# Coupling phase rewritten: twice-projected first state, two sequences in step, outputs by diagonal gate matmuls, steps placed by a table

## The reference, cut to what matters

```python
h = _layernorm(x) * (1 + cb) + sb
gf = _global_net(h.mean(axis=1))                 # per sequence one number, three small layers
out = h
for _ in range(3):                               # NUM_CYCLES
    tf = sigmoid(gelu(gelu(gelu(out @ w1 + b1) @ w2 + b2) @ w3 + b3) @ w4 + b4)   # 256 -> 256 -> 128 -> 64 -> 1
    coupling = 0.1 + r * ((0.7 * gf + 0.3 * tf) - 0.5) * 2.0      # one number per token
    o_r, o_i, p_r, p_i = split(out, 4)
    out = out + coupling * concatenate([p_r, -p_i, -o_r, o_i])    # the twist
x = x + gb * out
```

## Time and profile before

| | us |
|---|---|
| median of 3 runs (1328.81 to 1330.93) | 1330.33 |
| the profiled execution's own time | 1328.92 |
| its span, first to last instruction | 1327.0 |
| coupling phase in it, from the end of the last linear-attention add at 1066.8 | 260.2 |

### The profile page before, as it was taken

The page is one execution under the profiler, slowest core; times in us unless marked ns, Lnnn a source line. Parts: engine busy times, 40 slices in busy tenths (PEclk is TensorE's granted clock), DMA queues, the critical chain, the costliest instruction groups (busy, mean ns, idle before and its releaser), DMA issues. The chain is left out here.

```text
span 1327.0 us, 19347 instructions
## 1 busy us (share of the span) xinstructions
PE 1121.3 (84%) x6462; PEld 593.2 (45%) x6462; DVE 744.3 (56%) x1538; ACT 566.0 (43%) x1025; POOL 457.4 (34%) x668
## 2 busy tenths in 40 slices
PE   6279999999999991598989638999999929999996
PEld 5134445554544430354545315666666613333332
DVE  3167778788787745223223237777777623464543
ACT  0227676676776661123223213333333204545543
POOL 0345446445454310478877523222223100000000
PEclk7669999999999995699999859999999969999997
DMA  4134134233252213266666430111110020012000
GB/s 169 30 58 77 26 70 93 46 75 85 39 90 58 43 50 105 72 128 155 130 151 132 75 99 1 37 37 37 37 41 17 21 91 1 8 56 64 0 32 32
DMA packets 73042, 85.26 MB, mean 64 GB/s; under 512 B 12520, under 2 KB 67560, under 8 KB 72688
## 3 DMA queue, kind: packets, MB, share of 16 engines
q1 hardware_dynamic: 60656, 67.23, 19.8%
q0 software_dynamic: 12288, 16.79, 7.7%
HBM read 45.54 MB, written 25.47 MB: 54 GB/s over the span
## 5 line engine op out<-in xcount | busy, mean ns | idle before, releaser
L655 DVE TENSOR_REDUCE nmax<-psum 128x1 f32<-128x512 f32 (+3 forms) x352 | 215.5, 636 | 51.9 <-PE psum L847 46.5
L759 ACT ACTIVATE pT<-psum 128x512 f32<-128x512 f32 x320 | 181.1, 596 | 66.7 <-PE psum L866 36.6
L845 PE MATMUL psum<-k6T,q6T 96*128 96x512 bf16 (+3 forms) x512 | 128.2, 310 | 14.3 <-DVE nmax L655 10.2
L863 PE MATMUL psum<-q6T,k6T 99*128 99x512 bf16 x320 | 119.4, 382 | 1.1 <-ACT pT L759 0.9
L1084 POOL DMA_INDIRECT residual<-expert_y,idx_e x64 | 101.2, 1581 | 37.6 <-DVE expert_y L1206 21.1
L2029 PE MATMUL psum<-c_state,c_w 128*128 128x512 f32 x192 | 102.5, 636 | 0.1
L847 PE MATMUL psum<-negs_bf,ident_bf 128*128 128x128 bf16 (+2 forms) x352 | 88.8, 252 | 0.0
L845 PEld LDWEIGHTS psum<-k6T,q6T 96*128 96x128 bf16 x512 | 45.7, 99 | 88.0 <-DVE nmax L655 55.5
L878 PE MATMUL psum<-pT,v 128*32 128x512 f32 x640 | 85.1, 604 | 0.0
L1487 DVE TENSOR_TENSOR l_scores<-psum,const_sb 128x512 f32<-128x512 f32 x128 | 79.1, 679 | 10.0 <-PE psum L1639 10.0
L1071 POOL DMA_INDIRECT expert_tokens<-router_input,idx_e x64 | 63.7, 995 | 54.3 <-POOLq L947 35.2
(11 more groups left out here) (234 smaller groups left out, 2259.1 us busy)
## 6 DMA issues: line engine op xcount, KB each, us to landing
q6T<-q_parts SPq DMA_DIRECT2D x96, 128.0 KB, 4.5
expert_w<-in_ew SPq DMA_DIRECT2D x16, 768.0 KB
x_in<-in_x SPq DMA_DIRECT2D x8, 512.0 KB, 4.0
residual<-x SPq DMA_DIRECT2D x32, 128.0 KB, 1.8
router_input<-h SPq DMA_DIRECT2D x32, 128.0 KB, 1.8
l_x<-residual SPq DMA_DIRECT2D x8, 512.0 KB, 4.2
x_dram<-l_x SPq DMA_DIRECT2D x32, 128.0 KB, 3.5
c_x<-x_dram SPq DMA_DIRECT2D x4, 1024.0 KB, 6.0
```

What stands on the lines that cost most here:

```text
L655: dve.tensor_reduce(nmax[:, i, u * nh:(u + 1) * nh], ps_s[:, n % SR, 0:nh * (i + 1) * P].rearrange("p (h k) -> p h k", h=nh), AX_X, ALU.ma ...
L759: act.activation(pT[:, n % PR].rearrange("p h t -> p (h t)"), ps_t[:, n % TR, :], ACT.Exp, scale=HD ** -0.5).then_inc(probs, 1)
L845: pe.matmul(out[:, a, :], q6T[0:6 * HD, b % 2, u * nh + a, i * P:(i + 1) * P], k6T[0:6 * HD, b % 2, 0:w], start=a == 0, stop=False, skip_g ...
L863: last = pe.matmul(out, k6T[:, b % 2, j * P:(j + 1) * P], q6T[:, b % 2, hg * 4:hg * 4 + 4, i * P:(i + 1) * P], start=True, stop=j < i)
```

## The change

Only the coupling phase changes (and shared helpers: `attention_order` becomes `placed_order`, with the same table and order for attention; the signals that GpSimd primed in setup are gone). What it does now, per pair:

- `PR`: the first state `h` is multiplied by `w1` and by a twisted copy of it, `w1[:, 1]`, once: 2 sequences x 2 weights x 2 output halves, two matmuls each. ACT drains each into `pr` (and for the plain one also applies the gelu into `a1`). The layer-1 input of cycles 1 and 2 is made from `pr` by DVE in `up` (one scale, two products, two sums per sequence), with no L1 matmul; between them `r2` prepares the base of the third cycle.
- `L3` and `L4` of both sequences are issued together, on the two column halves and the two row halves of the array.
- `tok`: the coupling numbers are computed per token on partitions (four matmuls of two columns per cycle), `fin` turns them into alpha and beta of the third state by eleven small DVE operations.
- `oT`: for each of 8 token tiles, four real matmuls of the first state against diagonal gate matrices (`diag`, written by ACT), which transpose, gate and twist at once; DVE scales by alpha and beta and adds x.
- `xn` moves from DVE to ACT, and POOL gets two more small operations for its bias. The last cycle has no `L4` and no `up`.
- Steps stand where a table puts them, one period of 48 places per pair, and pairs overlap; there is no loop.

```diff
-def half_cycle(c1, a1, c2, a2, first=False, second=False):
-def coupling_prologue():
-def coupling_merged():
-class CouplingSignals:
+COUPLING_STEPS = 48
+COUPLING_PLACE = {
+    "ln": -143, "st": -136, "xn": -132, "diag": -116,
...
+}
@@ SP @@
+                        if q >= 3:
+                            sp.wait_ge(done, 2 * NT * (q - 2))
+                        sp.dma_start(x_in[:, q % 3], m.x3_d[...]).then_inc(in_loaded[q % 3], 16)
+                        if q == 0:
+                            (nine weight loads)
@@ POOL @@
+                        link(pool.tensor_scalar(vtmp[:], mv[:, :, 1], EPS, None, ALU.add))
+                        link(pool.tensor_tensor(rstd[:], vtmp[:], mhalf[:], ALU.pow))
+                        link(pool.tensor_tensor(vtmp[:], mv[:, :, 0], rstd[:], ALU.mult))
+                        pool.tensor_scalar(nbias[:], vtmp[:], -1.0, None, ALU.mult).then_inc(nbias_ready, 1)
@@ DVE @@
-                        chain.link(dve.tensor_scalar(cc[:, a, :], th[:, a, :], ...))
-                        dve.scalar_tensor_tensor(out=uv[:, a, 0, :], in0=st[:, 1, :], scalar=sgn, in1=cc[:, a, :], ...)
-                        chain.link(dve.scalar_tensor_tensor(out=uv[:, a, 1, :], in0=st[:, 0, :], scalar=nsgn[:, 0:1], ...))
-                        for k in range(KC):
-                            dve.tensor_tensor(st[:, k, :], st[:, k, :], uv[:, a, k, :], ALU.add)
+                        link(dve.tensor_scalar(cc[:, a, :], th[:, a, :], half[:, 2:3], coef[:, q % 2, a:a + 1], ALU.mult, ALU.add))
+                        dst = tmp[:] if c else pre[:, a]
+                        steps = [signed(dve.tensor_tensor(dst[:, k, :], pr[:, q % 2, a, 1, k, :], cc[:, a, :], ALU.mult))
+                                 for k in range(KC)]
+                        for k in range(KC):
+                            dve.wait_ge(dve_steps, steps[k])
+                            base = pre[:, a, k, :] if c else pr[:, q % 2, a, 0, k, :]
+                            dve.tensor_tensor(pre[:, a, k, :], base, dst[:, k, :], ALU.add).then_inc(pre_ready, 1)
+                    if s[0] == "r2":
+                        link(dve.tensor_tensor(tmp[:], pr[:, q % 2, a, 0], cc[...].to_broadcast([P, KC, T]), ALU.mult))
+                        link(dve.tensor_tensor(pr[:, q % 2, a, 1], pr[:, q % 2, a, 1], tmp[:], ALU.subtract))
+                    if s[0] == "oT":
+                        link(dve.scalar_tensor_tensor(out=ot[:, q % 2, n, :], in0=ps_o[:, n % 2, 0:C], scalar=al3[:, i, a:a + 1],
+                                                      in1=x_in[:, q % 3, n, :], op0=ALU.mult, op1=ALU.add))
+                        dve.scalar_tensor_tensor(out=ot[:, q % 2, n, :], in0=ps_o[:, n % 2, C:2 * C], scalar=be3[:, i, a:a + 1],
+                                                 in1=ot[:, q % 2, n, :], op0=ALU.mult, op1=ALU.add).then_inc(done, 1)
@@ ACT @@
+                        for i in range(2 * NT):
+                            ins = act.activation(xn[:, i, :], x_in[:, q % 3, i, :], ACT.Identity, bias=nbias[...], scale=rstd[...])
+                    if s[0] == "diag":     (eight of)
+                                act.activation(diag[:, q % 3, a, k, :], ident, ACT.Copy, scale=cols[:, 4 + k, a:a + 1])
+                    if s[0] == "PR":
+                        if w == 0:
+                            act.activation(a1[:, q % 2, a, h, :], src, ACT.Gelu, bias=bias[:, h:h + 1])
+                        act.activation(pr[:, q % 2, a, w, h, :], src, ACT.Copy).then_inc(pr_drain, 1)
@@ PE @@
-                        ins = pe.matmul(ps_1[:, a, h, :], w1[:, k, h * P:(h + 1) * P], o[:, q.s, a, k, :], ...)
+                            last = pe.matmul(ps_1[:, n % 2, :], w1[:, w, k, h * P:(h + 1) * P], o[:, q % 3, a, k, :], ...)
+                        for a in range(2):
+                            pe.wait_ge(l2, l2_use[("L2", q, c, a)] + 1)
+                            last = pe.matmul(ps_3[64 * a:64 * a + 64, :], w3[:], a2[:, a, :], tile_position=(0, 64 * a))
+                        for a in range(2):
+                            pe.matmul(ps_2[:, a, :], w4[64 * a:64 * a + 64, :], a3[64 * a:64 * a + 64, :], tile_position=(64 * a, 0))
+                        for i in range(NT):
+                            last = pe.matmul(ps_t[:, 2 * i:2 * i + 2], a3[:, i * P:(i + 1) * P], w4pair[:], start=True, stop=True)
-                                last = pe.transpose(ps_dve[...], og[:, a, k, ...], ident)
+                                last = pe.matmul(ps_o[:, n % 2, (KC * w + k) * P:(KC * w + k + 1) * P],
+                                                 o[:, q % 3, a, 1 - k if w else k, i * P:(i + 1) * P], diag[:, q % 3, a, KC * w + k, :])
```

More of the change, by code:

```diff
@@ L78, in shape_constants @@
     return c
[L81 to L104, removed]
 def settle(eng, passed):
     eng.sem_inc(passed, 1)
[L113 to L133, removed]
-S_HEADS = [4, 2, 1, 1]
[L148 to L160, removed]
+S_HEADS = [4, 2, 1, 1]
+ATTENTION_STEPS = 136
+ATTENTION_PLACE = {
     "ln": -197,
@@ L181, with placed_order, place @@
 }
+def placed_order(table, count, steps, sequences):
+    def place(s):
+        at = table[s[0]]
+        for n in s[1:]:
+            at = at[n]
+        return at
+    assert len(steps) == count
+    order = [(count * b + place(s), (s[0], b) + s[1:]) for b in range(sequences) for s in steps]
+    return [s for _, s in sorted(order)]
 def attention_steps():
@@ L1858, in _ @@
+                    if s[0] == "oT" and s[2] % 2:
+                        _, q, n = s
+                        sp.wait_ge(done, 2 * NT * q + n + 1)
+                        sp.dma_start(m.out_t[q * 2 * NT + n - 1:q * 2 * NT + n + 1].rearrange("i p c -> p i c"),
+                                     ot[:, q % 2, n - 1:n + 1]).then_inc(store[q % 2], 16)
+                for s in range(2):
+                    sp.wait_ge(store[s], 16 * NT * (R // 2))
             @block.gpsimd
             def _(pool):
-                chain = Chain(pool, g.pool_steps, m.passed)
@@ L1862, in step @@
[L1862 to L1871 removed]
+                count = [0]
@@ L1938, in _ @@
                 dve.tensor_scalar(half[:, 2:3], bias[:, 8:9], 0.3, None, ALU.mult)
[L1939 to L1942 removed]
+                dve.tensor_scalar(half[:, 3:4], bias[:, 8:9], 0.7, None, ALU.mult).then_inc(ready, 1)
+                dve.wait_ge(ready, 2)
+                for s in order:
+                    step(s)
@@ L1991, in _ @@
-                act.wait_ge(ready, 1)
-                program(act, step)
+                        _, q, c = s
+                        for a in range(2):
+                            act.wait_ge(l4_fill, 4 * q + 2 * c + a + 1)
+                            act.activation(th[:, a, :], ps_2[:, a, :], ACT.Tanh, bias=half[:, 0:1], scale=0.5).then_inc(l4, 1)
+                    if s[0] == "tok":
+                        _, q, c = s
+                        act.wait_ge(tok_fill, CYCLES * q + c + 1)
+                        if q:
+                            act.wait_ge(fin, q)
+                        act.activation(tht[:, c].rearrange("p i a -> p (i a)"), ps_t, ACT.Tanh, bias=half[:, 0:1],
+                                       scale=0.5).then_inc(tok, 1)
@@ new lines, in step @@
+                        last.then_inc(x_fill, 1)
+                    if s[0] == "g":
+                        if s[2] == 1:
+                            for k in range(KC):
+                                last = pe.matmul(ps_x[:, 0:2], g1w[:, k, :], sums[:, k, :], start=k == 0, stop=k == KC - 1)
+                        if s[2] == 2:
+                            last = pe.matmul(ps_x[0:64, 0:2], g2w[:], gs1[:], start=True, stop=True)
+                        if s[2] == 3:
+                            last = pe.matmul(ps_x[:, 0:2], g3w[:], gs2[:], start=True, stop=True)
+                        last.then_inc(x_fill, 1)
@@ L2065 @@
+                pe.wait_ge(ready, 2)
+                for s in order:
+                    step(s)
 INPUTS = {
```

545 lines of the change are left out of this document (283 added, 262 removed).

## The result

| | before | after |
|---|---|---|
| median of 4 runs each, us | 1330.37 (1328.81 to 1330.93) | 1291.24 (1290.34 to 1294.09) |
| profiled execution, its span | 1328.92, 1327.0 | 1294.09, 1292.3 |
| from the coupling phase's first DMA issue to the end | 258.1 | 217.6 |
| one pair's global net to the next's, undisturbed | 53.95 | 43.36 |

The ratio is 0.9711, 95% interval 0.9694 to 0.9729: 39 us faster. The forecast was 22 us faster, 1308, with a range from 1294 to 1327. The sign was right, the size too small, and the time lies just under the range. The profiled execution is the slowest of the four; its phases ahead of this one took 5.7 us longer than in the earlier trace rows, with PE at half clock for 3.4 us at 1017.3 and again at 1051.4.

What follows compares the result with a forecast made beforehand. The prediction took PE to bound the middle and latency chains both ends; start 1066.8 + lead-in 48.2 + middle 142.5 + tail 48 = 1305.5 us of span, 1307.4 with time outside it, stated as 1308, range 1294 to 1327.

Steps and rivals of the forecast that it cites:

- The middle: Stretch between the first L4 of the first and last pairs: three periods of 48.4 us less 2.7, 142.5 us.
- PE's sum of 47.8 a pair: PE's work for one pair in the middle, added up from prices per step: 47.8 us, before a 0.6 us wait.
- wait of the last L3: In a pair's last cycle, L3 needs the gelu soon after its L2: 0.6 us uncovered, making the period 48.4.
- the prediction's part on a rule: On PE, L1, L3 and L4 each follow another tile shape; a change of shape was put at some 0.15 us.
- The tail: After the last pair's first L4, nothing fills PE and the clock is mostly low: taken as 48 us.
- all at the high clock 41: Alternative for the end of the phase: 41 us in place of 48 if PE's clock stays high throughout.
- The lead-in: From the phase's start at 1066.8 to the first L4: 48.2 us, with first hT near 1087.
- The middle's missing tiles: The first period in the middle lacks two output tiles of an earlier pair: 2.2 us less.
- No gain from the pairs: Rival: paired L3 and L4 passes, or drains between shapes, come one after the other: 1323 us, chance 0.12.
- DVE's queue: Rival: DVE's second update behind r2 and output tiles comes late, 8 us uncovered in each period: 1332 us, chance 0.12.
- The clock: Rival: two drops of PE's clock a period in the middle, 3.4 us more each period: 1319 us, chance 0.10.
- Better ends: Rival: tail at the high clock (-7) and oT at the price of transposes (-4): 1297 us, chance 0.08.

Runs made afterwards that it cites:

- e1: The changed kernel with w3 and w4 zero-padded to 128x128, so L3 and L4 of the two sequences run one after the other: 1300.11 us, ratio 0.9748.
- e5: The kernel before with the L3 and L4 weights zero-padded to 128x128, so a half cycle has no change of tile shape: 1321.54 us, ratio 0.9937.
- e8: e6 with the two small layers of the global net also zero-padded to 128x128: 1286.34 us, ratio 0.9668.
- e3: The kernel before with the gelu passes behind L1, L2 and L3 over 256 of 512 columns, the rest zero: 1330.69 us, ratio 0.9974.
- e2: The changed kernel with each twisted w1 projection computed twice, eight more 512-column matmuls a pair: 1316.89 us, ratio 0.9864.
- e9: e5 with tanh and DVE's coupling pass also cut to 256 of 512 columns: 1319.41 us, ratio 0.9911.
- e4: The changed kernel with the gelu passes after layers 1, 2 and 3 over 256 of 512 columns, the rest zero: 1287.86 us, ratio 0.9647.
- e6: The changed kernel with the first pair's statistics ahead of DVE's wait for weights, and xn_ready signalled per sequence: 1287.36 us, ratio 0.9665.
- e7: The changed kernel with pairs 137 places apart in place of 48, so that no two overlap: 1401.84 us, ratio 1.0526.

## Why the prediction was off, step by step

Against the sum 1066.8 + 48.2 + 142.5 + 48 of the prediction, the profiled execution has 1072.5 (5.7 more, outside of the change) + 49.7 + 128.9 + 41.2 = 1292.3.

**The middle, 13.6 too much: the step that failed is PE's sum of 47.8 a pair.** The mechanism was right: PE bounds, and no other engine holds it. The prices were taken from a stream of single matmuls that alternate in shape and carried this alternation, and the waits of that order, with them:

| term | priced | after, by count |
|---|---|---|
| eight PR | 14.6 | 13.7 |
| six L2 | 12.5 | 10.3 |
| eight oT | 8.8 | 7.1 |
| three tok | 3.3 | 2.4 |
| hT, g | 3.3 | 2.6 |
| five L3/L4 pairs | 5.3 | 4.3, and 2.3 around changes of shape |
| wait of the last L3 | 0.6 | 0.7 |
| period | 48.4 | 43.4 |

The terms of after are counts times the distance in a run of equals: the matmuls of 512 columns at 0.857 (eight L2 records in 3.44 and the like: 33 a pair, 28.3), `hT` 4 x 0.43, `oT` 8 x 0.89, `tok` 3 x 0.81, and the global net 0.9: 40.4, so 3.0 of the period are lost between them, 0.7 of it at the one wait. (By the plain distances to the next start, PR has 14.2, L2 10.6, oT 7.6, and the pairs with the wait 5.8, where 5.9 was priced.) The same count for before is 48 x 0.857, `hT` 2.0, output transposes 2.0 and the global net 1: 46 of 53.95, so 8 us were lost. I read the earlier trace rows as prices of steps: L2 2.08, L1 1.82 for four, all else 1.05. They were prices of steps and of what stood around them. Two things were in them. A change of shape, nearly 0.2 us, four in a half cycle (e1 and e5 show it from both sides, e8 one by itself), and waits: L2 for the second gelu of L1 (e3 shows 0.19 for it), L1 for the update. In the new order the eight L2 records stand in one run whose inputs are long there, and there are ten changes of shape a pair besides the global net's, not 24.

I had in fact seen the change of shape (0.15 in the prediction's part on a rule) and then neither took it out of PR's 1.82 nor counted it in the new order. L2's surplus, 0.36 a step, is two waits, its own and that of the L1 behind it. `oT` was priced by four records that stood behind a wait of 0.47, and `tok` by twice a group's length of 0.61, which is not a distance: it contains the last record's run to its end. The page "TensorEngine Tiling (Array Packing)" of the Trainium skill, section "Key Properties", says that changing the tiling mode drains TensorE. The runs agree that a change costs time: some 0.2 us each in e1, e5 and e8.

Part by part the period went from 53.95 to 43.36: sixteen PR matmuls in place of 24 of L1 are 6.8 less (e2), the two L4 that the last cycle no longer has about 2, the pairs 2.35 (e1); outputs cost 5.1 more and `tok` 2.4. These come to some -3.6. The remaining 7 us are time that the old order lost between its matmuls, and of it the forecast gave back 2 only. The kernel before stood close to three limits at once in each half cycle: PE with its changes of shape (8.0), the loop over tanh and update (7.65, e5), and the hand-offs to ACT behind single matmuls (7.4, e9). So removing the first gave 0.4 a half cycle; the new order, with two pairs in flight, gets clear of them together. Counted over the starts of single records, the pair of before from 1199.36 to 1253.32 loses 4.2 at 24 changes of shape, 1.1 at L2's second gelu, 0.7 before L1, 1.5 at `hT` (whose steps share one bank and wait for its drain) and the rest around the global net. This says where PE stood, not what the removal of one would give: of the 4.2, e5 got back 1.7 a pair, since other waits grew.

**The tail, 6.8 too much.** Its own parts were right: L2 waits for the update's gelu, 5.3 us after L4 as forecast, and the second sequence's L2 comes at 8.7 where 8.5 was forecast. The clock was the step that failed. I took it as low from the second L2 on, since before ended that way; it fell for two stretches of 3.4 us only, each behind an idle wait of 1.5 and 3.15 us, and was at full level again for `tok` and the outputs. The last 41.2 us have 0.92, where those of before have 0.82 (0.65 in its last 21). In the other versions of the new order with pairs overlapped (e1, e2, e4, e6, e8) the tail has the lower level for 3.4 to 8.2 us, so this part of the time differs from profile to profile. I had named this, "all at the high clock 41", and gave it too little weight.

**The lead-in, 1.5 too little.** The weights landed 8.6 after the first DMA, not 7.1, and ACT's eight `xn` took 4.04, not 2.8, so the first `hT` came 2.7 later in the phase than forecast. The terms from there to the first L4 add up to 1116.1 in the prediction, not 1115, so 29.1; measured 26.8. The two misses in part cancel. e6 removes the first cause and gains 5.2.

**The middle's missing tiles, 1.6 the other way.** The first period lacks 0.7, not 2.2.

**The rivals.** No gain from the pairs: fell (e1, and L3's four records in 1.01), but nearly half of it was true, 1.9 of the 4.3 of a period is given back. DVE's queue: fell; PE idles for 0.8 us in three periods (41.86 busy of 42.64, then none), and the wait that its busy time hides, 0.7 a period, is for ACT. DVE's wide `r2` passes took 1.22, not 1.37, and the four passes of an update ran without gaps between them. The clock: fell, 1.00 in the middle. Better ends: half right, and right in sign for both of its parts, tail and `oT`; a case in which all of PE's prices in the middle are lower was missing among them.

## What to carry to other kernels

Before you price new work by the spacing of old records, ask what part of the spacing is a wait or a change of tile shape: take a matmul's price from a run of equals whose inputs are ready (here 0.43 a record of 512 columns, 0.11 of 128), and add shape changes and waits by count. If all engines are under 60% but PE is busy for 97% of a stretch, count the columns: what they don't account for is the order's, and a new order can recover it. Put waits for weights behind the work that doesn't need them, and signal halves where the consumer needs halves.

## What was not expected of the hardware

- A change of tile shape costs nearly 0.2 us of PE: 0.73 for the four of a half cycle before, 0.19 for the one that e8 takes away, beside a matmul of two columns. Zero-padding a 64-wide weight to 128x128 made the kernel before 8 us faster for no other edit (e5).
- A matmul that waits for its input starts 0.05 after the end of the pass that it waits for (L2's second half, L3 and L4 in e9), and its second record comes 0.10 later than in a run of equals: a start that is 0.08 late costs 0.19. Waits of this size don't show as idle time of PE.
- PE's clock fell in the tail for 3.4 us behind a wait of 1.5 us and again behind one of 3.15 us, and came back both times; idle waits of 0.78 and 1.16 us later in the tail had no such fall; with pairs apart (e7) the same work ran at clock 0.79.
- Two row or column halves of 64 run side by side with float32 and 512 columns: four records in 1.01 us, where the same on full tiles took 1.82.
